# Value products of 512 columns in every second slot of a decoder layer, with a new table of slots

## What is computed

```
x = x + attn(layernorm(x))            # 16 heads of 16, rotary positions, softmax over 512 keys
x = x + xattn(layernorm(x), context)  # causal self attention + attention over the context, summed
x = x + ffn(layernorm(x))             # 16 experts, top 1, capacity 256 tokens each
```

## Time and profile before

| | |
|---|---|
| median of 3 runs | 1619.16 us (1611.63 to 1634.64) |
| profiled execution | span 1626.3 us, 37857 instructions |
| mean granted TensorE clock | 0.963 |
| TensorE busy | 1443.6 us (89%) |
| VectorE busy | 1204.3 us (74%) |
| ScalarE busy | 1062.0 us (65%) |
| POOL busy | 650.5 us (40%) |
| attention bodies | about 51 to 59 us each, 24 of them |

### The profile page before, as it was taken

How to read it: one execution, slowest core, us unless ns; L and a number is a source line. 1 busy time by engine, 2 the same in 40 slices (tenths; PEclk the granted TensorE clock), 3 DMA queues, 4 the chain that set the end, 5 groups by cost and what they waited for, 6 DMA issues and landing times.

```text
span 1626.3 us, 37857 instructions
## 1 busy us (share of the span) xinstructions
PE 1443.6 (89%) x14610; PEld 647.8 (40%) x14610; DVE 1204.3 (74%) x2434; ACT 1062.0 (65%) x2139; POOL 650.5 (40%) x535
## 2 busy tenths in 40 slices
PE   3799999999999898898998989989989978779997
PEld 1222322333333433334334244333343432359997
DVE  6788878888876776776877877768778677537774
ACT  2377777778777676676676676766766656425662
POOL 2544565466422422236145333352352211225554
PEclk8699999999999999999999999999999999889999
DMA  6435344444323433323323322332333211157771
GB/s 179 115 119 141 105 112 115 120 115 112 92 60 95 110 88 101 90 83 104 82 83 88 104 80 69 96 98 71 85 100 97 60 45 39 48 189 262 251 259 62
DMA packets 119479, 175.82 MB, mean 108 GB/s; under 512 B 26273, under 2 KB 85895, under 8 KB 114696
## 3 DMA queue, kind: packets, MB, share of 16 engines
q1 hardware_dynamic: 111376, 158.50, 34.4%
q0 software_dynamic: 5888, 14.24, 2.7%
q10 hardware_dynamic: 2048, 0.83, 0.2%
HBM read 102.33 MB, written 51.18 MB: 94 GB/s over the span
## 4 chain that ended last, share of the span: by engine, by line
PE 54%; DVE 17%; DMA 9%; ACT 6%; issue 6%; POOL 5%; SPq 2%; POOLq 0%; DVEq 0%; ACTq 0%
PE psO L741 13%; PE psM L466 9%; PE psS L764 9%; DVE negmax L1193 9%; PE psK L466 6%; PE psK L795 6%; PE psS L466 4%; ACT probs L1029 4%; DMA recipB<-recip_scratch 3%; PE psK L693 2%; DVE xn L1165 2%; DMA shared<-shared 1%; DVE stats L1141 1%; DMA stack<-mrows 1%; PE psM L831 1%
## 5 line engine op out<-in xcount | busy, mean ns | idle before, releaser
L1193 DVE TENSOR_REDUCE negmax<-psS 128x1 f32<-128x512 f32 (+3 forms) x1536 | 869.4, 615 | 273.6 <-PE psS L764 136.4
L1029 ACT ACTIVATE probs<-psK 128x512 f32<-128x512 f32 (+3 forms) x1536 | 753.7, 544 | 325.3 <-PE psK L795 198.4
L741 PE MATMUL psO<-probs,V 128*32 128x256 f32 (+1 forms) x5632 | 446.1, 389 | 23.8 <-ACT U L1021 17.8
L764 PE MATMUL psS<-stack 48*128 48x512 f16 (+3 forms) x1536 | 284.5, 367 | 57.2 <-DVE negmax L1193 53.7
L795 PE MATMUL psK<-stack 50*128 50x512 f16 (+3 forms) x1536 | 278.5, 359 | 26.1 <-DMA stack<-mrows 14.7
L764 PEld LDWEIGHTS psS<-stack 48*128 48x128 f16 x1536 | 74.2, 93 | 373.2 <-DVE negmax L1193 290.7
L741 PEld LDWEIGHTS psO<-probs,V 128*32 128x32 f32 x5632 | 113.5, 109 | 210.9 <-issue 122.8
L1427 POOL TENSOR_TENSOR rstd<-lnt,minus_half 128x4 f32<-128x4 f32 x24 | 24.7, 1028 | 193.1 <-DVE lnt L1157 193.1
L795 PEld LDWEIGHTS psK<-stack 50*128 50x128 f16 x1536 | 76.5, 95 | 57.4 <-ACT probs L1029 23.6
L1553 POOL DMA_INDIRECT out_dram<-stack,put_to x32 | 76.8, 2399 | 17.8 <-issue 9.1
L1441 POOL CAST shared<-shared 128x512 f16<-128x512 f32 x8 | 4.9, 612 | 191.2 <-ACT shared L1051 191.2
(11 more groups left out here) (192 smaller groups left out, 2063.1 us busy)
## 6 DMA issues: line engine op xcount, KB each, us to landing
spare<-in_L_ffn_w_dram SPq DMA_DIRECT2D x32, 1024.0 KB, 6.3
parts_scratch<-parts SPq DMA_DIRECT2D x192, 128.0 KB
stack<-parts_scratch SPq DMA_DIRECT2D x96, 256.0 KB, 4.0
stack<-parts_scratch SPq DMA_DIRECT2D x96, 128.0 KB, 4.2
packed<-U SPq DMA_DIRECT2D x192, 64.0 KB
recipB<-recip_scratch SPq DMA_DIRECT2D x48, 256.0 KB
shared<-shared SPq DMA_DIRECT2D x48, 128.0 KB, 2.1
probs<-back_scratch POOLq DMA_DIRECT2D x16, 258.0 KB, 3.1
```

The costliest lines, as they stand in the source:

```text
L741: mm = nc.tensor.matmul(psO[32 * i:32 * i + 32, q0:q1], v_of(par)[:, kt, 2 * g + i % 2 + PAIRS * (i // 2), :], probs[:, (unit + i % 2) % P ...
L764: mm = nc.tensor.matmul(psS[:, banks[hh], 0:n], stack_of(par, 0)[rows, hp, qt * P:(qt + 1) * P], stack_of(par, 1)[rows, hp, 0:n], start=Tr ...
L1029: nc.scalar.activation(probs[:, t % P_RING, i, q0:T], psK[:, S_BANKS[t][i], q0:T], ACT.Exp, scale=SM_SCALE / (1 if b.kind == "A" else WSCA ...
L1193: nc.vector.tensor_reduce(negmax[:, g % 2, at:at + 1], psS[:, S_BANKS[u // 2][j], 0:n], AX_X, ALU.max, negate=True).then_inc(s["max_done"], 1)
```

## The change

The value product of a unit is issued whole, 512 columns (fewer in B), in the odd slot t for unit t-3; even slots have none. The copy of U moves one slot earlier (slots 9, 17, 25 and 1). All warm matmuls but `warm_rows` and those of the draining body go. The slot table is new: jobs lie in odd slots, except proj2 of AA (20), zT1 (22) and count0 (28) of CC; no job is spread over two slots; projections start behind the last stack load in A and B bodies; layer norm steps are at 1, 3, 6 and 8 in A and B, the routed batch's at 2, 4, 8 and 10.

```diff
-    "AA": {"v0": (1, 2), "v1": (3, 4), "xT0": (7,), "xT1": (8,), "proj0": (12,), "proj1": (15,), "proj2": (18, 20),
-           "proj3": (22, 23), "out0": (25,), "out1": (26, 27), "ln": (1, 3, 4, 6), "load": (2, 3, 6, 7, 8, 9, 10, 11),
-           "split": (8, 8), "lower": (19, 22, 26, 30), "store": (22, 23, 30, 31), "recip": 7, "norm": 13, "attn": 15, "bias": 1},
-    "AB": {"v0": (2,), "v1": (3, 4), "xT0": (7,), "xT1": (10,), "proj0": (14,), "proj1": (15,), "proj2": (18,), "proj3": (23,),
-           "out0": (26, 27), "out1": (31,), "ln": (2, 3, 5, 6), "load": (1, 2, 3, 5, 6, 8, 9, 10),
-           "split": (10, 11, 15, 17, 17, 23), "store": (16, 19, 20, 25), "recip": 5, "norm": 10, "attn": 18, "bias": 1},
-    "AC": {"v0": (0,), "v1": (2,), "ctxT0": (7,), "proj0": (10,), "proj1": (11,), "proj2": (14, 15), "proj3": (17, 18),
-           "out0": (22,), "out1": (30,), "load": (0, 3, 3, 6, 7, 9, 9, 10), "split": (8, 10, 12, 15, 18),
-           "store": (12, 14, 17, 20), "recip": 8, "norm": 12, "attn": 15, "bias": 0},
-    "BB": {"v0": (0,), "v1": (2,), "xT0": (8,), "xT1": (10,), "proj0": (14, 15), "proj1": (16,), "zT0": (14,), "zT1": (16,),
-           "proj2": (20,), "logits0": (18,), "proj3": (23,), "count0": (23,), "out0": (24, 25), "out1": (28,),
-           "ln": (2, 5, 6, 7), "load": (1, 2, 3, 6, 7, 8, 9, 10), "split": (10, 11, 14, 17, 20, 23), "store": (16, 18, 21, 25),
-           "recip": 7, "norm": 11, "attn": 16, "route": (10, 11, 12, 13), "chain": (14, 19, 20, 23, 24),
-           "scatter": (27, 27, 28, 28, 29, 30, 31, 31), "back": 13, "out": 17},
-    "CC": {"v0": (0, 1), "v1": (2,), "ctxT0": (7,), "proj0": (9,), "proj1": (10, 12), "proj2": (14, 15), "proj3": (17,),
-           "zT0": (19,), "zT1": (20,), "logits0": (22,), "out0": (24,), "count0": (27,), "out1": (28,),
-           "load": (1, 2, 3, 6, 7, 8, 9, 10), "split": (8, 10, 13, 15, 18), "store": (12, 14, 17, 20), "recip": 8, "norm": 11,
-           "attn": 20, "bias": 2, "route": (6, 9, 13, 15), "chain": (23, 25, 26, 28, 28), "exp": 24,
-           "scatter": (29, 29, 30, 30, 30, 31, 31, 31), "back": 16, "out": 15},
+    "AA": {"v0": (1,), "v1": (3,), "xT0": (9,), "xT1": (11,), "proj0": (15,), "proj1": (17,), "proj2": (20,),
+           "proj3": (23,), "out0": (25,), "out1": (31,), "ln": (1, 3, 6, 8), "load": (2, 3, 6, 7, 8, 9, 10, 11),
+           "split": (10, 12), "lower": (21, 24, 27, 29), "store": (24, 26, 29, 31), "recip": 7, "norm": 13, "attn": 15, "bias": 1},
+    "AB": {"v0": (1,), "v1": (3,), "xT0": (9,), "xT1": (11,), "proj0": (15,), "proj1": (17,), "proj2": (19,), "proj3": (23,),
+           "out0": (25,), "out1": (31,), "ln": (1, 3, 6, 8), "load": (1, 2, 3, 5, 6, 8, 9, 10),
+           "split": (10, 12, 16, 18, 20, 24), "store": (18, 20, 22, 26), "recip": 7, "norm": 13, "attn": 19, "bias": 1},
+    "AC": {"v0": (1,), "v1": (3,), "ctxT0": (7,), "proj0": (9,), "proj1": (11,), "proj2": (15,), "proj3": (17,),
+           "out0": (23,), "out1": (31,), "load": (1, 3, 3, 6, 7, 9, 9, 10), "split": (8, 10, 12, 16, 18),
+           "store": (12, 14, 18, 20), "recip": 8, "norm": 13, "attn": 15, "bias": 0},
+    "BB": {"v0": (1,), "v1": (3,), "xT0": (9,), "xT1": (11,), "proj0": (15,), "proj1": (17,), "proj2": (19,), "proj3": (23,),
+           "out0": (25,), "out1": (27,), "ln": (1, 3, 6, 8), "load": (1, 2, 3, 6, 7, 8, 9, 10),
+           "split": (10, 12, 16, 18, 20, 24), "store": (18, 20, 22, 26), "recip": 7, "norm": 13, "attn": 16},
+    "CC": {"v0": (1,), "v1": (3,), "ctxT0": (7,), "proj0": (9,), "proj1": (11,), "proj2": (15,), "proj3": (17,),
+           "zT0": (19,), "zT1": (22,), "logits0": (23,), "out0": (25,), "count0": (28,), "out1": (27,),
+           "load": (1, 2, 3, 6, 7, 8, 9, 10), "split": (8, 10, 12, 16, 18), "store": (12, 14, 18, 20), "recip": 7, "norm": 11,
+           "attn": 20, "bias": 2, "route": (2, 4, 8, 10), "chain": (24, 26, 27, 28, 29), "exp": 25,
+           "scatter": (30, 30, 30, 31, 31, 31, 31, 31), "back": 16, "out": 15},
...
-WARM_JOB = {"A": {5: 2, 7: 2}, "C": {25: 2}}
-WARM_END = {"AA": {6: 2}, "AB": {6: 2, 7: 2}, "BB": {6: 2, 7: 2, 30: 2}, "CC": {12: 3, 15: 2}}
...
         kind = self.kind if t >= 3 else self.prev
-        if not kind:
+        if not kind or t % 2 == 0:
             return None
-        half = (t + 1) % 2
-        unit = (t - 3 - half) % SLOTS
-        first = q_from(kind, unit % 8 // 2)
-        q0, q1 = max(first, half * T // 2), (half + 1) * T // 2
-        return (t < 3, unit, q0, q1, q0 == first) if q0 < q1 else None
+        unit = (t - 3) % SLOTS
+        return t < 3, unit, q_from(kind, unit % 8 // 2)
...
-            if t == 2 and b.prev:
+            if t == 1 and b.prev:
                 return NG - 1
-            return t // 8 - 1 if b.kind and t > 2 and t % 8 == 2 else None
+            return t // 8 - 1 if b.kind and t > 1 and t % 8 == 1 else None
...
-                    ago = {2: 0, 16: 6, 24: 6, 30: 4}.get(t)
+                    ago = {2: 1, 16: 7, 24: 7, 30: 5}.get(t)
...
-                            mm = nc.tensor.matmul(psO[32 * i:32 * i + 32, q0:q1], v_of(par)[:, kt, 2 * g + i % 2 + PAIRS * (i // 2), :],
-                                                  probs[:, (unit + i % 2) % P_RING, i // 2, q0:q1],
-                                                  start=kt == 0 and q0 == 0, stop=kt == TT - 1, skip_group_check=True)
+                            mm = nc.tensor.matmul(psO[32 * i:32 * i + 32, q0:T], v_of(par)[:, kt, 2 * g + i % 2 + PAIRS * (i // 2), :],
+                                                  probs[:, (unit + i % 2) % P_RING, i // 2, q0:T],
+                                                  start=kt == 0, stop=kt == TT - 1, skip_group_check=True)
...
-                    if t in b.warm_job:
-                        keep_warm(spare_bank(b, t), b.warm_job[t])
...
-                    if t in b.warm_end:
-                        keep_warm(spare_bank(b, t), b.warm_end[t])
```

More of the change, by code:

```diff
@@ L112, in __init__ @@
         self.ln_steps, self.load_slots = self.slots.get("ln", ()), self.slots.get("load", ())
-        self.warm_job = WARM_JOB.get(kind, {})
-        self.warm_end = WARM_END.get(self.form, {})
         self.warm_rows = {16: 3} if kind == "B" else {0: 3}
@@ L706, in keep_last @@
                         keep_warm(psS[:, 0, :], n)
-            def spare_bank(b, t):
-                need(pe, s["exp_done"], b.at("exp_done", 2 * t))
-                return psK[:, 3 - sum(S_BANKS[t]), :]
             pe.wait_ge(cst_in, 16)
@@ L729, in _ @@
                     if av:
-                        prev, unit, q0, q1, first = av
+                        prev, unit, q0 = av
                         par = np_ if prev else b.parity
                         g, kt = unit // 8, unit % 8 // 2
-                        if first:
-                            need(pe, s["exp_done"], b.at("exp_done", 0 if prev else 2 * unit + 4))
-                            if not prev and unit == 0:
-                                pe.wait_ge(s["v_out"], b.at("v_out"))
-                            if kt == 0:
-                                need(pe, s["av_out"], b.at("av_out", int(b.prev is not None) + g))
+                        need(pe, s["exp_done"], b.at("exp_done", 0 if prev else 2 * unit + 4))
+                        if not prev and unit == 0:
+                            pe.wait_ge(s["v_out"], b.at("v_out"))
+                        if kt == 0:
+                            need(pe, s["av_out"], b.at("av_out", int(b.prev is not None) + g))
                         for i in range(GH):
-                            mm = nc.tensor.matmul(psO[32 * i:32 * i + 32, q0:q1], v_of(par)[:, kt, 2 * g + i % 2 + PAIRS * (i // 2), :],
-                                                  probs[:, (unit + i % 2) % P_RING, i // 2, q0:q1],
-                                                  start=kt == 0 and q0 == 0, stop=kt == TT - 1, skip_group_check=True)
+                            mm = nc.tensor.matmul(psO[32 * i:32 * i + 32, q0:T], v_of(par)[:, kt, 2 * g + i % 2 + PAIRS * (i // 2), :],
+                                                  probs[:, (unit + i % 2) % P_RING, i // 2, q0:T],
+                                                  start=kt == 0, stop=kt == TT - 1, skip_group_check=True)
                         mm.then_inc(s["av_done"], 1)
@@ L1013, in _ @@
                         act.wait_ge(s["av_done"], b.at("av_done", b.av_count(t)))
-                        if t == 2:
+                        if t == 1:
                             used = b.at("packed_1")
```

## The result

The changed kernel takes 1638.5 us (median of 4 runs, 1629.1 to 1650.9), the one before in the same session 1622.5 (4 runs, 1611.6 to 1634.6): a ratio of 1.0108, with a 95% interval of 1.0056 to 1.0160. By the ratio that is 18 us slower (the medians differ by 16), where +8 was forecast. The profiled execution after is the fastest of its four (span 1627.3 us), so sums of its rows show less than the 18 us.

A forecast was written before the change was run, and what follows sets the result against it. TensorE leads but no engine is full; 4 to 6 us per body go to its waits. Terms -48 + 47 - 18 - 12 + 10 + 5 + 24 = +8 us on the profiled 1626.3; forecast 1628 us, own range 1600 to 1655.

The forecast's parts named there:

- the likeliest case: Whole kernel: time within 2% of before, chance 0.43; faster had 0.21 and slower 0.36.
- 512 columns: Value products: one of 512 columns takes 0.99 us where two halves took 1.14; 320 merges, -48 us.
- third rival: Value products: 512 columns cost as much as two halves, only the longer chain stays; 1676 us, chance 0.08.
- Lumping: Slot pairs with no job or a small one: 2.85 us instead of 2.43, 112 pairs, +47 us.
- The copy of U: Copy out of PSUM a slot earlier: value products no longer wait for ScalarE's copy, -18 us.
- Warm matmuls out: 152 warm matmuls removed: only the seven per C body, in slots with projections, save time, -12 us.
- The clock: TensorE's granted clock: about 20 more falls to 1.2 GHz, at 1.2 us each, +24 us.
- Layer norm, routing: Routing's last chain, slot 28 to 29 in seven C bodies, delays the next maxima: +10 us; layer norm steps unchanged.
- SP's queue: Six A bodies with A ahead: later lowering and swap DMAs make K(21) to K(24) 7.8 us against 6.94, +5 us.
- B's slots 7 to 17: B bodies: reciprocal to K(17) stays near 16 us, so TensorE's savings there go into that wait, 0.
- first rival: Whole kernel: TensorE's savings come through, 1570 us, between 1525 and 1590; chance 0.21.
- The second: Rival, slower by the clock: two falls more per body beyond the sum's, 1695 us, from 1650 up; chance 0.27.

The follow-up runs named there:

- with halves: The changed kernel with value products again in 256-column halves in every slot and U copied one slot later, new table, no warm matmuls: 1.0231 against before.
- the merged kernel: The kernel before with whole 512-column value products, old table and warm matmuls kept: 1.0367 against before; with the new table and warm matmuls: 1.0149.

## Why the prediction was right, and where its terms were not

The forecast of 1628 us, +8 on the profiled execution, met 1638 us and +18: the likeliest case, within 2% of before and on the slower side. By steps:

- **512 columns, -48 us:** right in its step. 1.00 us from start to S against 0.99. The third rival (two halves' cost) is out.
- **Lumping, +47:** the length after was right (2.82 us against 2.85), the price wasn't. The pair before is 2.83 us from K to K; the 2.43 us were taken from value half to value half, ahead of a wait of S for a maximum. The prediction's own lower bound, 0 "if the pair before really averaged 2.85", is what the rows show for this pair.
- **The copy of U, -18:** right. 3.7 us of idle time left in the row, and 28.5 of U's come back with halves. The three together, -19, were measured as -20. With the second term as it is, that agreement is in part luck: whole products gain more than 0.15 us in some pairs with a large job (0.48), and nothing is lost in those without.
- **Warm matmuls out, -12:** -3 us in the kernel before (0.9983, with no change inside its interval). It was priced without the clock, which had a term of its own.
- **The clock, +24:** real, mis-sized. 8 falls more were counted where I had expected 20; 13 us of it (give or take 10) come back when the gaps are filled.
- **Layer norm, routing, +10:** the 1.4 us per C body is seen, in place, but taking it back moved the total by 2 us, give or take 10.
- **SP's queue, +5:** K(21) to K(24) is 6.93 us, not 7.8, and undoing it gives 1 us.
- **B's slots 7 to 17, 0:** the step held as it was put (15.9 us against "near 16"), and was still wrong as a price: a cast two slots later is worth 17 us after and nothing before.
- **Missing: the floor.** The prediction priced the new places of the jobs at nothing. It named every wait behind the exponents and none from S over the maximum to S. By the runs, the old table would have cost the merged kernel 35 us more (part of it through the clock), and v0 and v1 in even slots alone cost 20.

The measured parts along one path are -3 (warm matmuls out), +40 (new table, halves) and -20 (merge); that they add up to the whole, +17, is by construction. The forecast for the same three is -12 + 24, +15 and -19. The merge fits as a sum; the table with the clock is where the missing 10 us lie. What in the table costs the halves 40 us is only partly known: the cast is a candidate that was shown with whole products only. So the total came out close because the parts leaned both ways: lumping was charged 47 us that it didn't cost, and the new table too little.

The first rival (TensorE's savings come through) fell: TensorE lost 75 us of busy time and the time rose. It fell by the floor and by the table, not by the longer pair that was argued against it. The second (1695 through the clock) fell: it asked for 48 falls more.

## What to carry to other kernels

Work out the shortest step of a software pipeline from its buffers: fill, read out the first, fill again, here 0.42 + 0.64 + 0.11 = 1.17 us with three banks and two filled per slot. Compare a step before and after between the same two instructions; a pair read from another point here promised 0.42 us that wasn't there. When work is lumped into every second slot, that floor stands bare in the others; one filler must lie in each interval, so the lumped product and the loose jobs belong on opposite sides of the refill. Price a layout and the table made for it together, by the four corners (old and new of each), since here the one cost 3.7% and the other 2.5% by themselves, and both together 1.1%. (The 3.7% are with warm matmuls, the others without: of neither square are all four corners measured.)

## What the hardware showed that was not expected

- Matmuls whose result nobody reads made the kernel faster where they lay in gaps: 256 more, 45 us more of busy time, 13 us less in all. The 152 of the kernel before gave nothing on balance, though there are 65 us more at 1.2 GHz without them.
- In the kernel before, no B body has a fall of the clock in its slots 8 to 12; with whole products and the same warm matmuls seven of eight have one in slot 8.
- Executions of one kernel differ by 1.3% (1629.1 to 1650.9 us after), those with the lower granted clock being the longer ones. A term of 5 or 10 us could be told from its local rows only, not from the total.
